# Expert stage of a four-layer network: tiles of 128 tokens, chunks of 256, and weighting dealt between the one-hot instructions

## The chip, the cores and the metric

The kernel runs on one core of one Trainium2 chip. A core has TensorE (PE, matrix products; its weight loads are PEld), VectorE (DVE), ScalarE (ACT), GpSimd (POOL) and SyncE (SP, which issues transfers). Each engine has its own list of instructions, in a written order, and engines wait for each other by semaphores. The metric is the device time of one execution in microseconds (us). The text calls TensorE's two clock levels 1.2 and 2.4 GHz; the profile writes them as a granted clock of 0.50 and 1.00.

## The reference, cut to what matters

The network has 3136 tokens (16 images of 14x14) of 256 channels and four layers. The change lies in the feed-forward part of the third. For each token and each of 8 heads it makes two lists of 64 scores, takes the 16 best of each, forms the sums of the candidates, takes the 16 best of those, and so picks 16 of 4096 experts for each head. Each expert is a row of `expert_down` and a row of `expert_up`.

```python
q = (x_norm @ wq).reshape(B, T, HEADS, 2, DIM_KEY)
sim = jnp.einsum('bthpd,hkpd->pbthk', q, keys)
s1, i1 = jax.lax.top_k(sim[0], K)
s2, i2 = jax.lax.top_k(sim[1], K)
all_idx = (i1[..., :, None] * NUM_KEYS + i2[..., None, :]).reshape(B, T, HEADS, K * K)
all_scores = (s1[..., :, None] + s2[..., None, :]).reshape(B, T, HEADS, K * K)
final_scores, pk = jax.lax.top_k(all_scores, K)
final_idx = jnp.take_along_axis(all_idx, pk, axis=-1)
hidden = jnp.einsum('btd,bthkd->bthk', x_norm, expert_down[final_idx])
hidden = jax.nn.gelu(hidden, approximate=False) * jax.nn.relu(final_scores)
out = jnp.einsum('bthk,bthkd->btd', hidden, expert_up[final_idx])
```

## The kernel before, in words

The whole stage is `peer_ffn` (lines 1353 to 1844). It gathers no rows of experts. It computes the product of every token with all 4096 experts, as 32 blocks (`J`) of 128, applies Gelu, and multiplies the result by a matrix of weights that is zero but for the picked experts. That matrix is built for each token as a product of one-hot matrices: 128 rows from the code `a`, 32 columns from the code `b`, the weight carried as a high and a low bf16 part.

The tokens come in 14 chunks (`CT`) of 224, each of two tiles (`TT`) of 112 tokens and four half tiles (`HT`) of 56 tokens. In a tile, tokens lie on partitions, so that one instruction of the search works on 112 tokens. In what follows chunk n is in work, and the codes of chunk n+1 are searched in the same time. The order on each engine, for chunk n:

- PE (line 1577): `hidden` for 10 of 16 pairs of blocks (L1516, 80 matmuls), then `turn` for both tiles, which transposes the codes (L1525) and waits for `codes_ready`, then `hidden` for the other 6 pairs (48), then `queries` of chunk n+1 (L1494, 16). Then `scatter` for half tiles 0 to 3 (L1540 and L1541, two matmuls for each token, so 112 for each), with `scores` of chunk n+1 (L1503, 8) behind half tile 0 and behind half tile 1. Last comes `experts_out` (L1550, 128).
- DVE (line 1827): `low_weights` (L1791), `one_hots` for half tiles 0 to 3 (four instructions each: L1808, L1809 and twice L1812) and `weigh` for half tiles 0 and 1 (L1820, four each, one for each quarter of a half tile). `weigh` stands behind `one_hots` of the next half tile and multiplies Gelu's result by the scattered weights in PSUM. Then `top_halves` for both tiles, `make_codes` (L1728 to L1786), and last the addition to `x` (L1843).
- ACT: Gelu (L1617), the copies of transposed codes (L1628 to L1630), queries and scores (L1597, L1603), and the copies of the scattered weights of half tiles 2 and 3 (L1639), which POOL multiplies in (L1482).

`one_hots` of half tile hb writes the buffers `oh_a[hb % 2]`, `oh_h[hb % 2]` and `oh_l[hb % 2]`, so it waits until PE has done the scatter of half tile hb-2 (`m_done`). `scatter` of a half tile waits for `oh_ready`, which the last of the four one-hot instructions sets. The function `chunks` (line 1433) writes out the first two and the last two chunks, and puts the others into a loop of two chunks for each turn.

Of the kernel before, what the change touches and what calls it, by code (L numbers as in the profile page):

```python
# [1352 lines left out]
def peer_ffn(nc, x, xn_dram, w, ident):  # L1353
# [10 lines left out]
    TT = 112  # L1364
# [8 lines left out]
    GT = HT // 4  # L1373
    LOWEST = -3.4028235e38
# [4 lines left out]
    with Scope(nc, "peer") as S:  # L1379
# [107 lines left out]
        def _(pe):  # L1487
            def queries(n, p):
# [3 lines left out]
                for m in range(4):  # L1492
                    for k in range(KC):
                        mm = nc.tensor.matmul(sim_ps[m // 2][:, (m % 2) * CT:(m % 2 + 1) * CT], wq[:, k, m * P:(m + 1) * P],  # L1494
                                              xc[p][:, k, :], start=(k == 0), stop=(k == KC - 1))
                mm.then_inc(q_done, 1)

            def scores(n, t):
# [731 lines left out]
```

## Time and profile before

| | |
|---|---|
| median of 3 runs | 2701.39 us (2698.59 to 2703.5) |
| the profiled execution, its own time | 2689.78 us |
| its span, first to last instruction | 2688.1 us |
| mean granted TensorE clock | 0.82 |
| busy: PE, PEld, DVE, ACT, POOL | 2236.6, 1940.0, 1847.0, 663.9, 435.8 us |
| 14 chunks of the expert stage, first transpose of codes to last addition | 676.0 to 2095.7 us |

The busy time of an engine is the union of its instructions. Matmuls are pipelined, so that a stretch in which PE is always busy may still hold more or fewer of them. Start times from instruction to instruction say more than durations. A stretch of the span is named by its start and end in us.

### The profile page before, as it was taken

What the parts mean: (1) busy time and instruction counts of PE and PEld (TensorE: products, weight loads), DVE (VectorE), ACT (ScalarE), POOL (GpSimd) and SP (SyncE); (2) the same over time, 40 slices, a digit from 0 to 9 for tenths busy, and PEclk for the clock granted to TensorE, in tenths of its full rate; (3) what the DMA queues carried; (4) which work ended last, traced back from release to release, by engine and by line L of the source; (5) the groups of instructions that cost most, each with busy time, mean ns of one, the idle gap of its engine ahead of it and who ended that gap; (6) DMA issues with size and microseconds to landing.
All of it is one profiled execution on the core that took longest, in us unless ns stands there. A gap on an engine that the chain in (4) does not pass through costs nothing. (4 is left out here: it accounts for less than half of the span.)

```text
span 2688.1 us, 50156 instructions
## 1 busy us (share of the span) xinstructions
PE 2236.6 (83%) x18017; PEld 1940.0 (72%) x18017; DVE 1847.0 (69%) x7732; ACT 663.9 (25%) x1527; POOL 435.8 (16%) x521
## 2 busy tenths in 40 slices
PE   6585999955989889989989889989888799648994
PEld 3464788734889788888989889889888577326663
DVE  4334666448889889898898898898895577440003
ACT  1432455432211111211211211111111255402220
POOL 2003444310101201102102012012012310030003
PEclk8777999966788697787787887887786799869996
DMA  1104444225000000000000000000000233042323
GB/s 53 34 18 98 106 108 99 47 73 118 5 4 1 5 5 2 5 5 2 5 1 5 5 1 5 5 1 5 1 1 1 65 83 81 7 165 82 104 92 102
DMA packets 87043, 107.85 MB, mean 40 GB/s; under 512 B 26222, under 2 KB 75502, under 8 KB 86062
## 3 DMA queue, kind: packets, MB, share of 16 engines
q1 hardware_dynamic: 81328, 96.62, 13.7%
q0 software_dynamic: 3296, 6.43, 0.9%
q8 instruction: 146, 2.39, 0.4%
q10 hardware_dynamic: 2176, 1.61, 0.2%
q14 instruction: 97, 0.79, 0.1%
HBM read 70.61 MB, written 30.51 MB: 38 GB/s over the span
## 5 line engine op out<-in xcount | busy, mean ns | idle before, releaser
L1540 PE MATMUL peer_x_ps<-peer_oh_h,peer_oh_a 128*128 128x32 bf16 x3136 | 417.2, 249 | 6.1 <-DVE peer_oh_l L1812 4.4
L1540 PEld LDWEIGHTS peer_x_ps<-peer_oh_h,peer_oh_a 128*128 128x128 bf16 x3136 | 414.2, 149 | 8.5 <-DVE peer_oh_l L1812 5.7
L1541 PE MATMUL peer_x_ps<-peer_oh_l,peer_oh_a 128*128 128x32 bf16 x3136 | 417.8, 249 | 0.0
L1541 PEld LDWEIGHTS peer_x_ps<-peer_oh_l,peer_oh_a 128*128 128x128 bf16 x3136 | 412.9, 149 | 3.6 <-issue 1.5
L1516 PE MATMUL peer_x_ps<-peer_xc,peer_dt 128*128 128x224 f32 x1792 | 374.4, 373 | 31.7 <-DMA peer_up<-in_L_ffn_expert_up_dram 19.4
L1482 POOL TENSOR_TENSOR peer_g<-peer_g,peer_qt 128x448 f32<-128x448 f32 x112 | 189.7, 1715 | 1275.0 <-ACT peer_qt L1639 1274.9
L1550 PE MATMUL peer_out_ps<-peer_g,peer_up 128*128 128x224 f32 x1792 | 370.9, 372 | 30.6 <-issue 28.4
L1516 PEld LDWEIGHTS peer_x_ps<-peer_xc,peer_dt 128*128 128x128 f32 x1792 | 362.1, 204 | 40.0 <-issue 34.6
L1550 PEld LDWEIGHTS peer_out_ps<-peer_g,peer_up 128*128 128x128 f32 x1792 | 361.1, 203 | 37.6 <-issue 32.4
L1617 ACT ACTIVATE peer_g<-peer_x_ps 128x448 f32<-128x448 f32 x224 | 121.9, 544 | 652.1 <-PE peer_x_ps L1516 652.1
L1277 DVE TENSOR_REDUCE l_attn_mx<-l_attn_s_ps 98x4 f32<-98x392 f32 (+1 forms) x320 | 175.0, 560 | 140.4 <-PE l_attn_s_ps L1047 100.6
L1808 DVE TENSOR_TENSOR peer_oh_a<-peer_a_t,peer_iota_f 128x7168 bf16<-128x7168 bf16 x56 | 217.6, 3886 | 1.4
L1662 DVE FIND_INDEX8 peer_i<-peer_v,peer_sc 112x8 uint32<-112x64 f32 x896 | 186.4, 220 | 0.0
L1198 ACT ACTIVATE l_attn_pt<-l_attn_st_ps 98x392 f32<-98x392 f32 x320 | 148.2, 492 | 151.2 <-PE l_attn_st_ps L1060 150.4
L2165 DVE TENSOR_TENSOR moe_y<-moe_y_ps,moe_b 98x256 f32<-98x256 f32 x32 | 13.6, 425 | 222.8 <-PE moe_y_ps L2039 222.8
L1043 PE MATMUL l_attn_s_ps<-l_attn_stk,l_attn_stq 96*98 96x196 bf16 (+1 forms) x768 | 112.8, 244 | 27.5 <-DMA l_attn_stk<-l_attn_pieces_k_dram 15.6
L1820 DVE TENSOR_TENSOR peer_g<-peer_g,peer_x_ps 128x448 f32<-128x448 f32 x112 | 67.6, 620 | 94.6 <-PE peer_x_ps L1541 94.5
L1657 DVE MAX8 peer_v<-peer_sc 112x8 f32<-112x64 f32 x896 | 118.7, 209 | 11.3 <-issue 10.1
L972 POOL TENSOR_SCALAR_AFFINE_SELECT l_attn_pt<-l_attn_pt 98x196 f32<-98x196 f32 (+1 forms) x192 | 98.5, 518 | 140.9 <-ACT l_attn_pt L1198 139.5
L1060 PE MATMUL l_attn_st_ps<-l_attn_stq,l_attn_stk 98*98 98x196 bf16 (+1 forms) x768 | 112.7, 245 | 10.2 <-ACT l_attn_pt L1198 4.4
L2039 PE MATMUL moe_y_ps<-moe_w,moe_h 128*98 128x256 f32 x512 | 111.8, 379 | 0.0
L2039 PEld LDWEIGHTS moe_y_ps<-moe_w,moe_h 128*98 128x98 f32 x512 | 84.5, 165 | 27.6 <-issue 1.3
(308 smaller groups left out, 3633.5 us busy)
## 6 DMA issues: line engine op xcount, KB each, us to landing
moe_w<-in_L_ffn_w_dram SPq DMA_DIRECT2D x16, 1024.0 KB, 9.1
l_attn_pieces_q_dram<-l_attn_pieces_q SPq DMA_DIRECT2D x16, 294.0 KB, 3.9
l_attn_pieces_k_dram<-l_attn_pieces_k SPq DMA_DIRECT2D x16, 294.0 KB, 3.1
l_attn_stq<-l_attn_pieces_q_dram SPq DMA_DIRECT2D x16, 294.0 KB
l_attn_stk<-l_attn_pieces_k_dram SPq DMA_DIRECT2D x16, 294.0 KB
peer_g<-n_L_ffn_expert_down_dram SPq DMA_DIRECT2D x8, 512.0 KB, 6.7
peer_up<-in_L_ffn_expert_up_dram SPq DMA_DIRECT2D x2, 2048.0 KB
l_xi<-net_x SPq DMA_DIRECT2D x16, 196.0 KB, 2.3
```

The lines of the kernel that those rows point to most:

```text
L1198: nc.scalar.activation(pt[g % NPT][:, f * FW:(f + 1) * FW], st_ps[i % 2][0:TH, 0:FW], ACT.Exp).then_inc(exp_done, 1)
L1277: nc.vector.tensor_reduce(mx[n % 2][:, hs[0]:hs[0] + len(hs), t], s_ps[i % 2][0:TH, 0:FW].rearrange("p (h j) -> p h j", j=nb * TH), AX_X, ...
L1482: nc.gpsimd.tensor_tensor(g[:, :, ts], g[:, :, ts], m_copy[q % 2].rearrange("p (t j) -> p j t", j=J), ALU.mult).then_inc(g_done_late, 1)
L1516: mm = nc.tensor.matmul(x_ps[b][:, jj * CT:(jj + 1) * CT], dt[:, k, 2 * jp + jj, :], xc[p][:, k, :], start=(k == 0), stop=(k == KC - 1))
L1540: nc.tensor.matmul(x_ps[q][:, i * J:(i + 1) * J], oh_a[hb % 2][:, :, t], oh_h[hb % 2][:, :, t], start=True, stop=False)
L1541: mm = nc.tensor.matmul(x_ps[q][:, i * J:(i + 1) * J], oh_a[hb % 2][:, :, t], oh_l[hb % 2][:, :, t], start=False, stop=True)
L1550: mm = nc.tensor.matmul(out_ps[:, m * CT:(m + 1) * CT], up[:, j, m * P:(m + 1) * P], g[:, j, :], start=(j == 0), stop=(j == J - 1))
L1617: nc.scalar.activation(g[:, 2 * jp:2 * jp + 2, :], x_ps[jp % 4][:, 0:2 * CT].rearrange("p (j t) -> p j t", j=2), ACT.Gelu).then_inc(gelu_d ...
L1657: ins = nc.vector.max(values[:, q, r], source)
L1662: last = nc.vector.max_index(indices[:, q, r], values[:, q, r], source)
L1808: nc.vector.tensor_tensor(view(oh_a[q]), spread(a_t, P), number(P), ALU.is_equal)
L2039: mm = nc.tensor.matmul(y_ps[s % 2][0:ST, 0:C], h[p][:, f, s * ST:(s + 1) * ST], w2[p][:, f, :], start=(f == 0), stop=(f == KF - 1))
```

## The change

Tiles have 128 tokens, half tiles 64, chunks 256. 3136 tokens are 12 such chunks and a rest of 64, which is a 13th chunk of one half tile: all functions are given the number of tokens of the chunk in work (`now`) and of the one that is searched (`then`). The loop holds chunks 2 to 9 (four turns; before, chunks 2 to 11 in five).

For room, the small buffers of `make_codes` (`t1`, `f16`, `step16` and others) now lie behind the selection matrices in `oh_a`. The wait for all scatters of the chunk in work (`m_done`) therefore stands at the head of `make_codes`, where it stood behind its search before.

The four `weigh` instructions of half tile hb-1 no longer follow `one_hots` of half tile hb. They stand between and behind its four instructions. The core of the diff:

```diff
-    TT = 112
+    TT = 128
...
+    REST = NT - NCHUNK * CT
...
-        f16, p16 = S.sb("f16", [TT, HH, TOP]), S.sb("p16", [TT, HH, TOP], U32)
-        t1, t2, t3 = S.sb("t1", [TT, PP]), S.sb("t2", [TT, PP]), S.sb("t3", [TT, PP])
+        def behind(p, word, words, dt):
+
+            o = TOP * PP + 2 * word
+            return flat[p][:, o:o + 2 * words].bitcast(dt)
+
+        t1, t2, t3 = (behind(0, i * PP, PP, F32) for i in range(3))
...
             for p in range(2):
-                chunk(NCHUNK - 2 + p, p, p == 1)
+                chunk(NCHUNK - 2 + p, p, CT, CT if p == 0 else REST)
+            chunk(NCHUNK, 0, REST, 0)
+
+        def tile_rows(tokens):
+
+            return [min(TT, tokens - t0) for t0 in range(0, tokens, TT)]
...
-            def chunk(n, p, last):
-                hidden(n, p, range(EARLY))
-                for t in range(NTILE):
-                    turn(n, t)
-                hidden(n, p, range(EARLY, NPAIR))
-                if not last:
-                    queries(n + 1, 1 - p)
-                for hb in range(NHB):
+            def chunk(n, p, now, then):
+                hidden(n, p, range(EARLY), now)
+                for t, rows in enumerate(tile_rows(now)):
+                    turn(n, t, rows)
+                hidden(n, p, range(EARLY, NPAIR), now)
+                if then > 0:
+                    queries(n + 1, 1 - p, then)
+                next_rows = tile_rows(then)
+                for hb in range(now // HT):
                     scatter(n, hb)
-                    if hb < NTILE and not last:
-                        scores(n + 1, hb)
-                experts_out(n)
+                    if hb < len(next_rows):
+                        scores(n + 1, hb, next_rows[hb])
+                experts_out(n, now)
...
-            def make_codes(n):
-
+            def make_codes(n, tiles):
+
+                heads, rows = len(tiles) * NH, tiles[0]
                 v = v16[:, :, :].rearrange("t (h w) a -> t w h a", w=2)
                 o = 0
                 chain.wait()
+                wait(dve, m_done, 4 * NHB * n)
...
-                wait(dve, m_done, 4 * NHB * n)
...
             def one_hots(n, hb):
+
+                def weigh_last(quarter):
+                    if 0 < hb <= LATE:
+                        weigh(n, hb - 1, quarter)
...
                 nc.vector.tensor_tensor(view(oh_a[q]), spread(a_t, P), number(P), ALU.is_equal)
+                weigh_last(0)
                 chain.step(nc.vector.tensor_tensor(view(oh_l[q]), spread(b_t, J), number(J), ALU.is_equal))
+                weigh_last(1)
                 chain.wait()
-                for dst, wt in ((oh_h, wh_t), (oh_l, wl_t)):
-                    ins = nc.vector.tensor_tensor(dst[q][:, :, :], oh_l[q][:, :, :], wt[:, ts].unsqueeze(1).broadcast_to([P, J, HT]), ALU.mult)
-                ins.then_inc(oh_ready, 1)
-
-            def weigh(n, hb):
-
-                for q in range(4):
-                    dve.wait_ge(m_done, 4 * NHB * n + 4 * hb + q + 1)
...
+                nc.vector.tensor_tensor(oh_h[q][:, :, :], oh_l[q][:, :, :], wh_t[:, ts].unsqueeze(1).broadcast_to([P, J, HT]), ALU.mult)
+                weigh_last(2)
+                nc.vector.tensor_tensor(oh_l[q][:, :, :], oh_l[q][:, :, :], wl_t[:, ts].unsqueeze(1).broadcast_to([P, J, HT]),
+                                        ALU.mult).then_inc(oh_ready, 1)
+                weigh_last(3)
+
+            def weigh(n, hb, q):
+
+                dve.wait_ge(m_done, 4 * NHB * n + 4 * hb + q + 1)
...
-                for hb in range(NHB - 1):
-                    one_hots(n, hb + 1)
-                    if hb < LATE:
-                        weigh(n, hb)
...
+                for hb in range(n_hb):
+                    if hb + 1 < n_hb:
+                        one_hots(n, hb + 1)
```

DVE, the first chunk before, from the one-hot instructions of half tile 1 to those of half tile 2 (the last numbers are partitions and elements; `x4` are four in a row):

```order
L1808 TENSOR_TENSOR peer_oh_a<-peer_a_t,peer_iota_f 128x7168
L1809 TENSOR_TENSOR peer_oh_l<-peer_b_t,peer_iota_f 128x1792
L1812 TENSOR_TENSOR peer_oh_h<-peer_oh_l,peer_wh_t 128x1792
L1812 TENSOR_TENSOR peer_oh_l<-peer_oh_l,peer_wl_t 128x1792
L1820 TENSOR_TENSOR peer_g<-peer_g,peer_x_ps 128x32x14 x4
L1808 TENSOR_TENSOR peer_oh_a<-peer_a_t,peer_iota_f 128x7168
L1809 TENSOR_TENSOR peer_oh_l<-peer_b_t,peer_iota_f 128x1792
```

The same place on DVE in the changed kernel, where L1833 to L1840 are the one-hot instructions and L1848 is `weigh`:

```order
L1833 TENSOR_TENSOR peer_oh_a<-peer_a_t,peer_iota_f 128x8192
L1848 TENSOR_TENSOR peer_g<-peer_g,peer_x_ps 128x32x16
L1835 TENSOR_TENSOR peer_oh_l<-peer_b_t,peer_iota_f 128x2048
L1848 TENSOR_TENSOR peer_g<-peer_g,peer_x_ps 128x32x16
L1838 TENSOR_TENSOR peer_oh_h<-peer_oh_l,peer_wh_t 128x2048
L1848 TENSOR_TENSOR peer_g<-peer_g,peer_x_ps 128x32x16
L1840 TENSOR_TENSOR peer_oh_l<-peer_oh_l,peer_wl_t 128x2048
L1848 TENSOR_TENSOR peer_g<-peer_g,peer_x_ps 128x32x16
L1833 TENSOR_TENSOR peer_oh_a<-peer_a_t,peer_iota_f 128x8192
L1848 TENSOR_TENSOR peer_g<-peer_g,peer_x_ps 128x32x16
```

The four multiplications of half tile 0 have moved up between the one-hot instructions of half tile 1, and those of half tile 1 up into half tile 2. The instruction that sets `oh_ready` (L1840) now stands behind three of them.

DVE, the end of the stage in the changed kernel, which is all of its work for the 13th chunk from the one-hot instructions on:

```order
L1833 TENSOR_TENSOR peer_oh_a<-peer_a_t,peer_iota_f 128x8192
L1835 TENSOR_TENSOR peer_oh_l<-peer_b_t,peer_iota_f 128x2048
L1838 TENSOR_TENSOR peer_oh_h<-peer_oh_l,peer_wh_t 128x2048
L1840 TENSOR_TENSOR peer_oh_l<-peer_oh_l,peer_wl_t 128x2048
L1848 TENSOR_TENSOR peer_g<-peer_g,peer_x_ps 128x32x16 x4
L1875 TENSOR_TENSOR net_x<-net_x,peer_out_ps 128x2x64
```

Here the four multiplications stand together, and the addition covers 64 tokens.

## Rows read from the trace of the kernel before

**Rows 1.** Waits of the expert stage, 680 to 2030: us in total, times, longest.

```profile
DVE peer_g L1820 <- PE peer_x_ps L1541: 89.8, 71, 3.3
PE peer_tr_ps L1525 <- DVE peer_codes L1786: 73.2, 12, 8.1
```

**Rows 2.** DVE's stages: us, busy PE, PEld, DVE, ACT, POOL (instructions), clock, DMA, GB/s.

```profile
1192.89:1227.49 34.60, 33.45 (x304) 31.98 (x305) 26.27 (x23) 6.50 (x16) 0.00 (x0) 0.75 0.03 8
1227.49:1235.75 8.26, 8.26 (x101) 7.64 (x101) 8.22 (x5) 2.48 (x5) 3.34 (x2) 0.71 0.00 0
1235.75:1263.42 27.67, 25.46 (x206) 24.76 (x205) 27.41 (x265) 3.00 (x6) 10.21 (x7) 0.69 0.01 2
1263.42:1266.48 3.06, 3.06 (x18) 3.06 (x17) 2.99 (x10) 0.00 (x0) 0.00 (x0) 1.00 0.00 0
1266.48:1280.39 13.91, 11.09 (x51) 10.22 (x50) 13.75 (x133) 0.00 (x0) 0.00 (x0) 0.87 0.02 4
1280.39:1295.76 15.37, 15.36 (x73) 14.68 (x71) 15.04 (x29) 4.90 (x9) 0.00 (x0) 0.89 0.00 1
```

**Rows 3.** The same chunk by PE's stages: us, PE busy (instructions), clock, DMA, GB/s.

```profile
1192.89:1195.45 2.56, 1.41 (x7) 0.50 0.00 0
1195.45:1205.96 10.51, 10.51 (x50) 0.86 0.01 2
1205.96:1208.99 3.03, 3.03 (x17) 1.00 0.31 76
1208.99:1216.36 7.37, 7.37 (x113) 0.70 0.01 2
1216.36:1219.35 2.99, 2.99 (x12) 0.59 0.00 0
...
1229.66:1244.57 14.91, 14.91 (x225) 0.59 0.01 2
1244.57:1246.78 2.21, 0.00 (x1) 0.50 0.00 0
1246.78:1274.26 27.48, 27.48 (x128) 0.89 0.01 2
1274.26:1295.75 21.49, 18.67 (x81) 0.84 0.01 2
...
1298.69:1307.78 9.09, 9.09 (x50) 1.00 0.01 2
```

**Rows 4.** PE over 13 chunks and over the last one.

```profile
676.00:2016.67 1340.67, 1209.14 (x9646) 0.80 0.01 3
2016.67:2095.70 79.03, 69.05 (x630) 0.71 0.00 1
```

**Rows 5.** DVE timeline, one-hot instructions of half tile 3: start, us.

```profile
1227.49 3.88 DVE L1808 TENSOR_TENSOR peer_oh_a<-peer_a_t,peer_iota_f 128x7168 bf16<-128x7168 bf16 x1
1231.29 1.08 DVE L1809 TENSOR_TENSOR peer_oh_l<-peer_b_t,peer_iota_f 128x1792 bf16<-128x1792 bf16 x1
1232.41 1.09 DVE L1812 TENSOR_TENSOR peer_oh_h<-peer_oh_l,peer_wh_t 128x1792 bf16<-128x1792 bf16 x1
1233.42 2.40 DVE L1812 TENSOR_TENSOR peer_oh_l<-peer_oh_l,peer_wl_t 128x1792 bf16<-128x1792 bf16 x1
```

**Rows 6.** POOL timeline in the same stretch: start, us, how many, idle before.

```profile
1232.41 10.71 POOL L1482 TENSOR_TENSOR peer_g<-peer_g,peer_qt 128x448 f32<-128x448 f32 x6 [88.37 <-ACT peer_qt L1639]
```

**Rows 7.** DVE by form, two stretches: the same shape on 112 and on 98 partitions.

```profile
L1757 DVE TENSOR_TENSOR peer_t<-peer_t 112x256 f32<-112x256 f32 x11 | 4.6, 419 | 0.0
L2165 DVE TENSOR_TENSOR moe_y<-moe_y_ps,moe_b 98x256 f32<-98x256 f32 x10 | 4.2, 425 | 93.6 <-PE moe_y_ps L2039 93.6
```

**Rows 8.** PE timeline: 80 matmuls of `hidden` where no loop turns.

```profile
1374.74 15.30 PE L1516 MATMUL peer_x_ps<-peer_xc,peer_dt 128*128 128x224 f32 x80
```

**Rows 9.** PE, L1571 alone (16 matmuls, 128 weights, 128 columns, f32): us, busy, clock last.

```profile
618.01:619.65 1.64, 1.64 (x16) 1.64 (x15) 1.00 0.00 0
```

**Rows 10.** PE, L1043 alone (98 weights side by side, 98 columns, bf16).

```profile
249.00:249.19 0.19, 0.18 (x4) 0.18 (x3) 1.00 0.61 186
```

More of the change, by code:

```diff
@@ L1618, in hidden_out, with chunk @@
                                          ACT.Gelu).then_inc(gelu_done, 1)
-            def chunk(n, p, last):
+            def chunk(n, p, now, then):
                 wait(act, out_done, n)
-                hidden_out(n, range(EARLY))
-                for t in range(NTILE):
+                hidden_out(n, range(EARLY), now)
+                for t, rows in enumerate(tile_rows(now)):
                     act.wait_ge(tr_done, NTILE * n + t + 1)
-                    ts = slice(t * TT, (t + 1) * TT)
+                    ts = slice(t * TT, t * TT + rows)
@@ L1636, in chunk @@
-                for k in range(4 * (NHB - LATE)):
+                    nc.scalar.activation(wh_t[:, ts], tr_ps[:, 2 * TT:2 * TT + rows], ACT.Copy)
+                    nc.scalar.activation(a_t[:, ts], tr_ps[:, 0:rows], ACT.Copy)
+                    nc.scalar.activation(b_t[:, ts], tr_ps[:, TT:TT + rows], ACT.Copy).then_inc(tr_ready, 1)
+                hidden_out(n, range(EARLY, NPAIR), now)
+                if then > 0:
+                    query_out(n + 1, then)
+                    for t, rows in enumerate(tile_rows(then)):
+                        score_out(n + 1, t, rows)
@@ L1637, in chunk @@
+                for k in range(4 * max(0, now // HT - LATE)):
                     act.wait_ge(m_done, 4 * NHB * n + 4 * LATE + k + 1)
@@ L1702, in fold, with top_halves @@
                 else:
[L1703 to L1705 removed]
+                    chain.step(nc.vector.tensor_tensor(out, m[:, 0, :], m[:, 1, :], ALU.add))
+            def top_halves(n, t, rows):
                 dve.wait_ge(sim_ready, NTILE * n + t + 1)
@@ L1823, in _, with chunk @@
             for t in range(NTILE):
[L1824 to L1828 removed]
+                top_halves(0, t, TT)
+            make_codes(0, tile_rows(CT))
+            def chunk(n, p, now, then):
+                if p == 0 and now == CT:
                     chain.turn(n, 2)
[L1830 removed]
+                tiles, n_hb = tile_rows(now), now // HT
+                low_weights(n, 0, tiles[0])
                 one_hots(n, 0)
[L1832 to L1840 removed]
+                if len(tiles) > 1:
+                    low_weights(n, 1, tiles[1])
+                for hb in range(n_hb):
+                    if hb + 1 < n_hb:
+                        one_hots(n, hb + 1)
+                if n_hb == 1:
+                    for q in range(4):
+                        weigh(n, 0, q)
+                if then > 0:
+                    for t, rows in enumerate(tile_rows(then)):
+                        top_halves(n + 1, t, rows)
+                    make_codes(n + 1, tile_rows(then))
```

143 lines of the change are left out of this document (66 added, 77 removed).

## The prediction

> **What bounds the kernel now.** I read the waits of the expert stage first, then one chunk cut into DVE's stages, then the same chunk cut into PE's. The waits point both ways [rows 1]: PE waits for DVE's codes, 73.2 us in 12 waits, and DVE's `weigh` waits for PE's scatter, 89.8 us in 71. So neither engine is the bound by itself. The stages show a circle through both [rows 2, 3]. From the first transpose of the codes (1192.89) PE sets the pace: transposes 2.56, the rest of `hidden` 10.51, queries 3.03, scatter of half tile 0 7.37, scores 2.99, scatter of half tile 1 7.4. DVE has its one-hot matrices ready beside it, and ends the last `weigh` at 1227.49, about 0.8 behind the scatter. From there DVE sets the pace alone: one-hots of half tile 3 (8.26, they wait for the buffer that scatter 1 frees), the search in the halves (27.67), candidates (3.06), their search (13.91), codes (15.37). The circle is 34.60 + 68.27 = 102.87 us. All 13 intervals take 1340.67 us, 103.1 each, and what follows the last transposes 79.03 [rows 4]: 1419.7 us in all. PE's own work ends earlier than the codes, which is why it waits.
>
> **The change, part by part.**
>
> *Search on 128 partitions.* The instructions, their count and their elements per partition are the same; only partitions go from 112 to 128. The same shape takes 419 ns on 112 and 425 ns on 98 partitions [rows 7], so partitions cost nothing, and the 27.67 + 3.06 + 13.91 + 15.37 = 60.0 us stay 60.0 us for a chunk that is 8/7 as large. This is the gain. The buffers that now lie in `oh_a` are read and written at the same sizes; I charge nothing.
>
> *One-hot matrices of 64 tokens.* Everything on DVE that grows with tokens: 7168 elements start 3.80 us before the next instruction (1231.29 less 1227.49) and 1792 elements about 1.1 [rows 5]. One seventh more of both, fixed part left out, is 0.53 + 3 x 0.13 = 0.93 us a half tile. The last instruction took 2.40 instead of 1.09, 1.31 more, while POOL worked [rows 5, 6]. POOL now has its first work about 5.2 us after that half tile begins (4.92 before, plus a longer quarter of scatter and copy), and the two multiplications start at 5.6 and later, so that either one or both meet it. A meeting costs 1.31 to 1.5. Bounds 9.2 (no longer meeting than now) and 10.9 (two); I take 10.2.
>
> In rows 5 and 6 POOL's first instruction starts with one DVE multiplication and the next one is the long one. The Trainium skill ("SBUF — State Buffer", section "SBUF: two separate sides") says that a DVE instruction with two SBUF inputs and a GpSimd instruction reading SBUF lock each other out for the whole instruction. By that rule both multiplications would be held, 10.9 instead of 10.2, or 8 us more over the stage; the row shows one held of two in the old spacing, so the midpoint stands.
>
> *PE's part of the circle.* Matmuls of 256 columns instead of 224 and 128 instead of 112 for each half tile: hidden, queries and two scatters grow by 1/7. In rows 3, 9.09 us (clock 1.00) against 10.51 (0.86) is `hidden` without and with the clock lost in the wait for codes. With the level kept: transposes 2.7, hidden 10.4, queries 3.46, scatter 2 x 8.42, scores 3.1 (256 columns before and after), tail 0.85: 37.4. With it lost, 38.8. PE will idle about 3 us instead of 9 there, so I take 37.9. The circle is 37.9 + 10.2 + 60.0 + 0.2 = 108.3 us for 256 tokens, where 103.1 x 8/7 would be 117.8.
>
> *Weighing dealt between the one-hots.* I cost it at nothing. `weigh` of quarter q cannot start before that quarter is scattered, and `one_hots` of half tile 2 cannot start before scatter 0 has ended, since it reuses its buffer. Both ends are PE's. Let scatter 0 start at S. The dealt `weigh` instructions run at about S+2.3, 4.4, 6.5 and 8.6 with one-hot work between them, and DVE is free for half tile 2 at S+9.3, dealt or not. The waits of rows 1 stay, they only stand between other instructions. The price is in `oh_ready`: half tile 1 was ready before the scatter began, and now at S+8.4, behind three waits. Queued behind it is the scatter of half tile 1, which PE reaches after scores at S+11.5: 3.1 us of cover, without which each us late costs 12 us in all. Half tile 2 is ready 3.1 us ahead likewise; half tile 3 (10.2 after scatter 1 and its tail 0.85) is due 11.5 after it, margin 0.5, and is not on DVE's chain. Bounds: 0 and 1 us a chunk.
>
> *The wait for `m_done` moved to the head of `make_codes`.* PE ends scatter 3 at 1244.57, DVE begins there at 1263.42 [rows 2, 3]; afterwards the ends are some 20 us and 38 us behind scatter 1. 18 us of cover: nothing. The wait for `tr_done` stays.
>
> *PE becomes nearly as long as DVE.* From scatter 1's end: 37.1 + scores 3.1 + scatters 17.0 + POOL's last product 2.4 + experts_out 30 (27.48 less the 3.3 it loses at half clock, by 8/7, plus 3.3, and a us less in most chunks) + 80 hidden 17.3 = 106.9, against 108.3. The wait for codes shrinks to some 1.4 us. At a loop's turn PE loses more: `hidden` took 21.49 us from 1274.26 to 1295.75 instead of 15.30 [rows 3, 8], 6.2 more, 2.8 of it idle (21.49 less 18.67) and the rest clock (0.84). I take 5.3, since a shorter idle costs less clock. That was hidden by the wait for codes. Now 106.9 + 5.3 = 112.2 exceeds 108.3 by 3.9. There are three such turns (four before), 12 us. Bounds: 2.2 and 5 each.
>
> *The last, small chunk.* Chunk 11 searches only 64 tokens (half the instructions), so PE bounds it: 37.1 less 1.7 for short queries, no second scores, 17.0 + 2.4 + 30, then 80 matmuls with 64 columns. The trace has none; 128 columns with 128 weights take 1.64/16 = 0.10 us [rows 9], and 98 weights with 98 columns in bf16 0.047 [rows 10]. I take 0.109 (0.05 to 0.21, the half clock): 8.7. Sum 93.5. Then transposes and copies 1.6, one-hots 8.0, one scatter 8.4, `weigh` 0.9, 128 such matmuls 14 and a start at half clock 2.4, addition 0.3: 35.5 after 79.03.
>
> *Sum.* 11 x 108.3 + 12 + 93.5 + 35.5 = 1332.3 us against 1419.7: 87.4 less. The profiled execution of 2689.78 would become 2602.4. It lies 11.6 under the median of the runs shown, so for the median 2701.4 - 87.4 = 2614 us.
>
> **The rivals.**
>
> *A faster circle.* The clock stays up, POOL meets one instruction, turns cost 2.2: 11 x 107.0 + 6.6 + 91 + 33 = 1307.6, 112 less, 2589. If, beyond that, dealing took DVE's waits out, 89.8 us less, 2500; what speaks against it is that PE's scatter ends them. Two in a hundred for the latter.
>
> *PE's turn in the circle.* PE idles less, but if it loses clock at more places or POOL ends late, it is at 112 in every chunk: 11 x 112 + 93.5 + 35.5 = 1361, 59 less, 2643. For it: only 1.4 us separates the engines. Against: a busier PE held 1.00 in `hidden` when it had not waited [rows 3].
>
> *The search pays for partitions.* Then the 60.0 us become 68.6, the circle 116.9, and the stage 1332 + 95 = 1427: nothing gained, 2709. Rows 7 speak against it; 3 in 100.
>
> *Slower: the scatter's weights.* L1540 loads 128 weights of `oh_a` whose step goes from 56 to 64 elements, 112 to 128 bytes. It takes 7.37/112 = 66 ns at a granted clock of 0.70 and 14.91/224 = 67 ns at 0.59 [rows 3], so array clock does not set its pace, and weights side by side take 0.19/4 = 47 ns [rows 10]. Something in fetching or issuing them does, and it might dislike the round step. From both sides: 47 ns, and 103 to 109 ns (rows 9) as the slow end. At 109 PE has 512 x 0.043 = 22 us more: 129 a chunk, 11 x 129 + 12 + 115 + 41 = 1587, 167 more, 2869. It decides from a chunk of about 116.2 us, that is from 66 + 18 = 84 ns. At 47 ns the circle would shorten by 256 x 0.019 = 5. For it: the unexplained 66 ns. Against: 112 bytes are already a jump at every element. I take 66, the row of the same instruction.
>
> Beside this: the Trainium skill ("SBUF — State Buffer", section "Door 1: The DMA port swizzle") states 16-byte lines and a penalty for each access that leaves one. By it both steps pay the same and this rival is void; no run so far shows a step of 128 bytes.
>
> **How the numbers follow.** My forecast with its own range (2590 to 2635) 0.68; faster circle below that 0.06; PE at 112 or thereabouts 0.16; search pays for partitions 0.03 (half of it within 0.2%, half slower); slower scatter 0.05; other things 0.02. The time is 2614, the range 2588 to 2646: it takes in the third case and leaves out the last three. A measurement of this kernel cannot tell less than about 0.2%, 5 us, from nothing. Faster 0.91, the same 0.03, slower 0.06.
>
> **What would show it.** In the changed kernel's profile: first transposes of codes every 108 us or so, 112 at a loop's turn; L1678, L1683 and L1685 at 209 to 220 ns on 128 partitions; 128 scatter matmuls in 8.4 us; DVE's waits in `weigh` about as long a chunk as before (7 us); PE's wait for codes down from 6.1 us each to under 2. Wrong would be: the scatter over 8.8 us, scatter 1 or 2 waiting for L1840, `hidden` at a clock under 0.9 everywhere, or DVE waiting less for PE with an earlier end of scatter 1.

## The result, and the profile after

| | before | changed |
|---|---|---|
| median of the runs (lowest to highest), us | 2699.99 (2695.79 to 2703.5), 4 runs | 2795.77 (2790.82 to 2804.15), 4 runs |
| profiled execution / its span, us | 2689.78 / 2688.1 | 2790.82 / 2789.1 |
| expert stage, first transpose of codes to last addition, us | 1419.7 | 1523.0 |
| mean start to start of a scatter matmul, ns | 65.7 | 98.6 |

The ratio is 1.0368, with a 95% interval of 1.0344 to 1.0392: 3.7% slower, where 3.2% faster was forecast. In the profiled executions the stage is 103.3 us longer and the spans differ by 101.0, so the loss lies in the expert stage.

The waits tell it first. These are those of the changed kernel, 660 to 2130 (engine, what, line, released by what: us in total, times, longest), beside [rows 1]:

```profile
DVE peer_g L1848 <- PE peer_x_ps L1559: 174.2, 96, 5.2
PE peer_tr_ps L1543 <- DVE peer_wl_t L1812: 15.4, 12, 1.3
```

PE waits no longer for the search: of the 73.2 us behind `codes` nothing is left, only 1.3 us a chunk behind `low_weights`, between two transposes. DVE waits twice as long for PE. The bound has gone over to PE altogether. What PE does with the time stands in one chunk cut into PE's stages (us, PE busy and instructions, clock, DMA, GB/s), beside [rows 3]:

```profile
1275.98:1278.27 2.29, 1.00 (x8) 1.00 0.00 0
1278.27:1288.47 10.20, 10.20 (x49) 1.00 0.01 2
1288.47:1291.92 3.45, 3.45 (x17) 1.00 0.29 76
1291.92:1304.48 12.56, 12.56 (x130) 0.61 0.01 1
1304.48:1308.03 3.55, 3.55 (x10) 0.50 0.00 0
1308.03:1320.65 12.62, 12.62 (x129) 0.64 0.01 1
1324.20:1349.60 25.40, 25.40 (x257) 0.57 0.01 1
1349.68:1352.07 2.39, 0.01 (x2) 0.50 0.00 0
1352.07:1381.75 29.68, 29.68 (x128) 0.93 0.01 1
1381.95:1401.98 20.03, 17.61 (x81) 1.00 0.01 3
```

In order: transposes, the rest of `hidden`, queries, scatter of half tile 0, scores, scatter 1, then scatters 2 and 3, the wait for POOL's last product, experts_out, and `hidden` of the next chunk with a loop's turn in it. Everything but the scatter and the loop's turn lies within half a us of the forecast (2.7, 10.4, 3.46, 3.1 for scores, 2.4, 30); the turn's `hidden` was forecast at 17.3 + 5.3 = 22.6 and took 20.03. A scatter of 128 pairs takes 12.6 us, not 8.42: 98 ns for a pair of a weight load and a matmul. The profile's page has them in groups, one for each of the two matmuls of a token, of which the first is shown, and DVE's large one-hot instruction (busy us, mean ns of one, idle before):

```profile
L1558 PEld LDWEIGHTS peer_x_ps<-peer_oh_h,peer_oh_a 128*128 128x128 bf16 x3136 | 619.9, 235 | 6.5 <-DVE peer_oh_l L1840 3.5
L1558 PE MATMUL peer_x_ps<-peer_oh_h,peer_oh_a 128*128 128x32 bf16 x3136 | 621.6, 291 | 3.4 <-DVE peer_oh_l L1840 3.4
L1833 DVE TENSOR_TENSOR peer_oh_a<-peer_a_t,peer_iota_f 128x8192 bf16<-128x8192 bf16 x49 | 216.6, 4420 | 1.3
```

The matmul has 32 columns and 128 weights, as before; what is new in it is the step at which the weights are read, 128 bytes instead of 112, and with it the step of the 32 moving columns. (LDWEIGHTS overlap each other and the matmuls, so I go by the start-to-start time of the pairs.) The sum follows: a chunk's PE work was forecast at 106.9 us, and 512 pairs at 98.6 - 66 = 32.6 ns more make 123.6; the intervals between the first transposes of two chunks measure 122.7 to 123.2, and 125.8 to 126.1 at the three loop turns.

Two other causes can be looked at in the same trace, the clock and DVE's writes. The first 2 us of scatter 0 lie wholly at one clock level and its second half and more at the other (us, PE busy and instructions, clock, DMA, GB/s):

```profile
1291.92:1293.92 2.00, 2.00 (x23) 1.00 0.00 0
1295.92:1304.00 8.08, 8.08 (x86) 0.50 0.00 0
```

From start to start the matmuls take 95 ns in the first and 98 in the second. The last chunk has one scatter with DVE nearly idle (us; busy PE, PEld, DVE, ACT, POOL; clock, DMA, GB/s):

```profile
2140.00:2152.96 12.96, 12.96 (x128) 12.84 (x128) 2.08 (x3) 0.00 (x0) 0.00 (x0) 0.50 0.00 1
```

That is 101 ns a pair (12.96/128) at half clock with DVE busy 2.08 of 12.96 us, and 98 at a clock of 0.61 to 0.64 with DVE at work. Neither the clock nor DVE's writes can be much of it.

The dealing, on DVE's timeline from the scatter of half tile 0 (start, us, instruction, idle before and its releaser):

```profile
1295.24 0.69 DVE L1848 TENSOR_TENSOR peer_g<-peer_g,peer_x_ps 128x512 f32<-128x512 f32 x1 [5.05 <-PE peer_x_ps L1559]
1295.85 1.22 DVE L1835 TENSOR_TENSOR peer_oh_l<-peer_b_t,peer_iota_f 128x2048 bf16<-128x2048 bf16 x1
1298.39 0.70 DVE L1848 TENSOR_TENSOR peer_g<-peer_g,peer_x_ps 128x512 f32<-128x512 f32 x1 [1.33 <-PE peer_x_ps L1559]
1299.01 1.22 DVE L1838 TENSOR_TENSOR peer_oh_h<-peer_oh_l,peer_wh_t 128x2048 bf16<-128x2048 bf16 x1
1301.49 0.69 DVE L1848 TENSOR_TENSOR peer_g<-peer_g,peer_x_ps 128x512 f32<-128x512 f32 x1 [1.27 <-PE peer_x_ps L1559]
1302.10 1.22 DVE L1840 TENSOR_TENSOR peer_oh_l<-peer_oh_l,peer_wl_t 128x2048 bf16<-128x2048 bf16 x1
1304.69 0.69 DVE L1848 TENSOR_TENSOR peer_g<-peer_g,peer_x_ps 128x512 f32<-128x512 f32 x1 [1.37 <-PE peer_x_ps L1559]
```

All four `weigh` end a wait for PE, with one-hot work between them, as forecast; `oh_l` of half tile 1 is ready at 1303.3, and its scatter begins at 1308.03.

### The profile page after: what moved, and what is told of

Read it like the earlier page. It is cut to its first block and busy times, and to the rows that moved or that the text cites. A ratio compares the mean times of both kernels' runs of the same rounds, so it can differ in the third digit from the quotient of the medians.

```text
span 2789.1 us, 48544 instructions
## 1 busy us (share of the span) xinstructions
PE 2410.7 (86%) x17712; PEld 2047.9 (73%) x17712; DVE 1750.2 (63%) x7060; ACT 658.0 (24%) x1478; POOL 413.2 (15%) x505
## 5 line engine op out<-in xcount | busy, mean ns | idle before, releaser
L1558 PEld LDWEIGHTS peer_x_ps<-peer_oh_h,peer_oh_a 128*128 128x128 bf16 x3136 | 619.9, 235 | 6.5 <-DVE peer_oh_l L1840 3.5
L1558 PE MATMUL peer_x_ps<-peer_oh_h,peer_oh_a 128*128 128x32 bf16 x3136 | 621.6, 291 | 3.4 <-DVE peer_oh_l L1840 3.4
L1559 PEld LDWEIGHTS peer_x_ps<-peer_oh_l,peer_oh_a 128*128 128x128 bf16 x3136 | 619.4, 236 | 5.9 <-issue 5.3
L1559 PE MATMUL peer_x_ps<-peer_oh_l,peer_oh_a 128*128 128x32 bf16 x3136 | 621.6, 289 | 0.0
L1569 PE MATMUL peer_out_ps<-peer_g,peer_up 128*128 128x256 f32 (+1 forms) x1664 | 386.8, 401 | 29.3 <-issue 26.2
L1534 PE MATMUL peer_x_ps<-peer_xc,peer_dt 128*128 128x256 f32 (+1 forms) x1664 | 352.5, 372 | 27.5 <-DMA peer_up<-in_L_ffn_expert_up_dram 19.7
L1500 POOL TENSOR_TENSOR peer_g<-peer_g,peer_qt 128x512 f32<-128x512 f32 x96 | 170.4, 1775 | 1335.7 <-ACT peer_qt L1660 1335.7
L1638 ACT ACTIVATE peer_g<-peer_x_ps 128x512 f32<-128x512 f32 (+1 forms) x208 | 119.1, 572 | 643.6 <-PE peer_x_ps L1534 643.6
L1833 DVE TENSOR_TENSOR peer_oh_a<-peer_a_t,peer_iota_f 128x8192 bf16<-128x8192 bf16 x49 | 216.6, 4420 | 1.3
L1848 DVE TENSOR_TENSOR peer_g<-peer_g,peer_x_ps 128x512 f32<-128x512 f32 x100 | 69.3, 693 | 185.2 <-PE peer_x_ps L1559 185.2
L1683 DVE FIND_INDEX8 peer_i<-peer_v,peer_sc 128x8 uint32<-128x64 f32 (+1 forms) x800 | 167.2, 221 | 0.0
L1043 PE MATMUL l_attn_s_ps<-l_attn_stk,l_attn_stq 96*98 96x196 bf16 (+1 forms) x768 | 113.1, 244 | 28.4 <-DMA l_attn_stk<-l_attn_pieces_k_dram 17.3
L1678 DVE MAX8 peer_v<-peer_sc 128x8 f32<-128x64 f32 (+1 forms) x800 | 106.9, 213 | 10.9 <-issue 9.8
```

Source lines behind the costliest of these rows:

```text
L1043: mm = nc.tensor.matmul(out[:, j, :], stq[n % NB][0:KS, spot(h), t * TH:(t + 1) * TH], stk[n % NB][0:KS, spot(h), 0:nb * TH], start=(j == ...
L1500: nc.gpsimd.tensor_tensor(g[:, :, ts], g[:, :, ts], m_copy[q % 2].rearrange("p (t j) -> p j t", j=J), ALU.mult).then_inc(g_done_late, 1)
L1534: mm = nc.tensor.matmul(x_ps[b][:, jj * CT:jj * CT + cols], dt[:, k, 2 * jp + jj, :], xc[p][:, k, 0:cols], start=(k == 0), stop=(k == KC - 1))
L1558: nc.tensor.matmul(x_ps[q][:, i * J:(i + 1) * J], oh_a[hb % 2][:, :, t], oh_h[hb % 2][:, :, t], start=True, stop=False)
L1559: mm = nc.tensor.matmul(x_ps[q][:, i * J:(i + 1) * J], oh_a[hb % 2][:, :, t], oh_l[hb % 2][:, :, t], start=False, stop=True)
L1569: mm = nc.tensor.matmul(out_ps[:, m * CT:m * CT + cols], up[:, j, m * P:(m + 1) * P], g[:, j, 0:cols], start=(j == 0), stop=(j == J - 1))
```

## The experiments

**The theory**: the step of the scatter's weights, 128 bytes, is what costs 33 ns a pair, and the rest of the change gains what was forecast. **The rivals**: the moving operand (`oh_h`, `oh_l`), whose step also became 128 bytes; the dealing; the larger tile or the moved buffers as such. The pads below widen a row's step in memory and move the buffers behind it; the same elements are written and read.

| run | tokens a tile | step of weights, of moving, bytes | `weigh` | ns a pair | stage, us | time against before [95%] |
|---|---|---|---|---|---|---|
| before | 112 | 112, 112 | behind | 65.7 | 1419.7 | 1 |
| changed | 128 | 128, 128 | dealt | 98.6 | 1523.0 | 1.0368 [1.0344, 1.0392] |
| e1 | 112 | 128, 112 | dealt | 90.9 | 1476.9 | 1.0199 [1.0164, 1.0234] |
| e2 | 128 | 132, 128 | dealt | 62.5 | 1310.7 | 0.9593 [0.9558, 0.9627] |
| e3 | 128 | 128, 132 | dealt | 90.4 | 1477.5 | 1.0210 [1.0176, 1.0245] |
| e4 | 128 | 128, 128 | behind | 98.6 | 1523.4 | 1.0361 [1.0333, 1.0390] |
| e5 | 128 | 132, 132 | dealt | 63.5 | 1313.7 | 0.9582 [0.9549, 0.9615] |
| e6 | 128 | 132, 128 | behind | 62.4 | 1314.8 | 0.9590 [0.9543, 0.9638] |
| e7 | 112 | 132, 112 | dealt | 65.2 | 1423.3 | 1.0002 [0.9985, 1.0020] |
| e8 | 112 | 144, 112 | dealt | 60.4 | 1405.8 | one run: 2683.72 us, before 2698.97 |
| e9 | 128 | 136, 128 | dealt | 63.6 | 1314.2 | 0.9606 [0.9561, 0.9652] |
| e10 | 112 | 160, 112 | dealt | 79.8 | 1462.7 | one run: 2719.66 us, before 2685.17 |
| e11 | 112 | 136, 112 | dealt | 65.1 | 1425.5 | one run: 2696.61 us, before 2685.17 |
| e12 | 128 | 144, 128 | dealt | 63.5 | 1313.6 | 0.9592 [0.9567, 0.9618] |

"ns a pair" is the mean start-to-start time of the scatter's matmuls in the profiled execution. A single run may lie half a per cent off (the runs of before beside e10 and e11 span 2670.75 to 2693.76 us), so for e8, e10 and e11 the pace and the stage are what is read.

**e1_step64_tiles112**: the changed kernel taken back to tiles of 112, with the step alone put to 128 bytes.

```diff
-    TT = 128
+    TT = 112
...
-        oh_a = [S.sb(f"oh_a{p}", [P, P, HT], BF16) for p in range(2)]
+        STEP_A = 64
+        oh_w = [S.sb(f"oh_a{p}", [P, P, STEP_A], BF16) for p in range(2)]
+        oh_a = [m[:, :, 0:HT] for m in oh_w]
...
-            chunk(NCHUNK, 0, REST, 0)
```

> Edit: the changed kernel put back to tiles of 112 and chunks of 224 (14 chunks, no rest), with the rows of oh_a kept 64 elements (128 bytes) apart, of which 56 are used. Theory 1 (the step of the scatter's weights): a scatter matmul starts every 99 ns instead of 66, a half tile takes 11.0 us instead of 7.4, a chunk 103.1 + 7.4 = 110.5 us or a little more, the time is 2700 + 14 x 7.4 = about 2805 us. Theory 2 (something about half tiles of 64 tokens: full PSUM banks, 128 partitions, the small 13th chunk): 66 ns and 2700 us. Theory 3 (the step of the moving operands oh_h and oh_l, which stays at 112 bytes here): 66 ns and 2700 us.

Measured: 90.9 ns, 1.0199. One scatter of 112 pairs, where before took 7.37 [rows 3]:

```profile
1211.18:1221.34 10.16, 10.16 (x114) 0.67 0.01 2
```

The step alone slows the scatter, at the old tile size. The time came out at 2734.83 us, where the expectation had 99 ns and 2805. The stage loses 57 us and not the whole 112 x 4 x 25 ns = 11.3 us a chunk, because before PE still had about 6 us a chunk of waiting for codes to give. But 90.9 is not 98.6: a part is missing.

**e2_weights_step66**: the changed kernel, weights off the step.

```diff
-        oh_a = [S.sb(f"oh_a{p}", [P, P, HT], BF16) for p in range(2)]
+        STEP_A = 66
+        oh_w = [S.sb(f"oh_a{p}", [P, P, STEP_A], BF16) for p in range(2)]
+        oh_a = [m[:, :, 0:HT] for m in oh_w]
...
-        flat = [oh_a[p][0:TT, :, :].rearrange("t r k -> t (r k)") for p in range(2)]
+        flat = [oh_w[p][0:TT, :, :].rearrange("t r k -> t (r k)") for p in range(2)]
```

(`GI = 8` columns of `iota_f` instead of 16, or 14 at tiles of 112, make room for the pad, here and in e3, e5, e6, e9, e10 and e12. DVE's one-hot instruction takes 4420 ns with either, and e3, which has the same 8 columns, stays slow.)

> Edit: the changed kernel with the rows of oh_a 66 elements (132 bytes) apart, 64 used; to make room iota_f holds 8 columns instead of 16 and is read twice as often by the one-hot comparison. Theory 1: the scatter is back at about 66 ns a matmul (8.4 us a half tile) and the time near my forecast, 2614 us, in any case 2590 to 2646. Theory 2: 99 ns, 12.7 us a half tile, 2796 us. Theory 3: the same as theory 2.

Measured: 62.5 ns, 0.9593, 4.1% faster than before. Four bytes more between two weights turn the change from a loss into a gain. The expectation had 66 ns and 2590 to 2646 us. The pace is a little better than that, and 2572.14 us lies below the range; before took 2685.21 us beside it, and 0.9593 of the 2699.99 us above is 2590. The same stages of one chunk of e2 as were shown of the changed kernel:

```profile
1192.06:1194.17 2.11, 0.91 (x7) 1.00 0.00 0
1194.17:1204.55 10.38, 10.38 (x51) 1.00 0.01 2
1204.55:1208.00 3.45, 3.45 (x17) 1.00 0.28 76
1208.00:1215.95 7.95, 7.95 (x129) 0.78 0.01 2
1215.95:1219.37 3.42, 3.42 (x11) 0.52 0.00 0
1219.37:1227.37 8.00, 8.00 (x130) 0.70 0.01 2
1230.92:1247.14 16.22, 16.22 (x257) 0.50 0.00 2
1249.52:1279.12 29.60, 29.60 (x129) 0.94 0.01 2
1279.12:1298.86 19.74, 17.54 (x82) 1.00 0.01 2
```

Only the scatter differs: 7.95 and 8.00 for 12.56 and 12.62, 16.22 for 25.40. It does so at clocks of 0.78, 0.70 and 0.50, at the same 62 to 63 ns a pair.

**e3_moving_step66**: weights at 128 bytes, the moving operand off the step.

```diff
-        oh_h = [S.sb(f"oh_h{p}", [P, J, HT], BF16) for p in range(2)]
+        oh_h = [S.sb(f"oh_h{p}", [P, J, 66], BF16)[:, :, 0:HT] for p in range(2)]
```

(and `oh_l` alike)

> Edit: the changed kernel with the rows of oh_h and oh_l (the scatter's moving operands, 32 columns) 66 elements apart and oh_a left at 64; iota_f of 8 columns as in the kernel with weights at 66. Theory 1: no change against the changed kernel, 99 ns and 2796 us, since weights are 128 of the 160 elements that a matmul fetches. Theory 3: 66 ns and about 2614 us. If both operands matter in proportion, some 93 ns and 2775 us.

Measured: 90.4 ns, 1.0210, which is e1's pace. One scatter of 128 pairs:

```profile
1169.75:1181.32 11.57, 11.57 (x129) 0.65 0.01 1
```

The expectation of the first theory, no change, failed: the moving operand's step costs 8 ns a pair too, and this is the part missing in e1, whose moving operand stayed at 112 bytes. So of the 33 ns, 25 come with the step of the weights alone (e1) and 8 with both steps at 128 bytes.

**e4_no_deal**: the changed kernel with `weigh` of half tiles 0 and 1 put back behind the next one-hots.

```diff
-                    if 0 < hb <= LATE:
-                        weigh(n, hb - 1, quarter)
+                    pass
...
+                        if hb < LATE:
+                            for q in range(4):
+                                weigh(n, hb, q)
```

> Edit: the changed kernel with the four weighing multiplications back behind the one-hot instructions of the next half tile, everything else as changed. Theory 1 and my account of the dealing (PE's scatter ends both orders): no change, 2796 us within 5. Rival, dealing costs time because oh_ready comes late and PE waits for it: 5 to 20 us less than the changed kernel. Rival, dealing saves time: more than 2800.

Measured: 1.0361 [1.0333, 1.0390] beside 1.0368 [1.0344, 1.0392] of the changed kernel; DVE waits 183.5 us in `weigh` over the span instead of 185.2. The dealing does nothing while PE is the bound.

**e5_both_step66** (the diffs of e2 and e3 together) and **e6_step66_no_deal** (those of e2 and e4).

> Edit: as the kernel with weights at 66 elements, and the rows of oh_h and oh_l 66 apart as well. So far: weights and moving operand both at 128 bytes 99 ns, moving operand alone moved off 91, weights alone moved off 62.5. If the two costs add up: 62.5 less 8 = about 54 ns a scatter matmul, and some 512 x 0.008 = 4 us less a chunk for PE. If the scatter is limited by something else once the weights are off 128 bytes: 62 ns and the time of the kernel with weights alone at 66, within 5 us.

> Edit: weights at 66 elements, and the weighing multiplications back behind the one-hot instructions. Here DVE and PE are within 1 to 2 us of each other in a chunk, so the dealing can show. My account (scatter ends both orders): the same time as with dealing, within 4 us, and the same wait of DVE for PE in a chunk. Rival, dealing pays because DVE's waits go: 10 us or more slower without it. Rival, dealing costs through the late oh_ready: 5 us or more faster without it.

Measured: 63.5 ns, 0.9582, and 62.4 ns, 0.9590; both intervals hold e2's 0.9593. So the moving operand's step costs something only when the weights' step is 128 bytes as well; an effect that adds up would have given 54 ns. And the dealing is worth nothing at the better step either: DVE idles 70.6 us before `weigh` without it and 70.4 with it.

**e7_tiles112_step66** (e1 with `STEP_A = 66`) and **e8_tiles112_step72** (`STEP_A = 72`).

> Edit: tiles of 112 and chunks of 224 as before, weights at 66 elements (132 bytes) instead of 56 (112 bytes), buffers and dealing as changed. If 132 bytes give 62.5 ns here as well, two scatters in the circle are 0.8 us shorter, the stage some 11 us, and the kernel is 0.4% faster than before. Then the tiles of 128 are worth some 97 us by themselves. If the pace of 62.5 came from the larger tiles: 66 ns and the time of before.

> Edit: as the kernel with tiles of 112 and step 66, but 72 elements (144 bytes). If only a step of a whole 128 bytes is slow: 62 to 66 ns. If the pace gets worse with the power of two in the step (112 and 144 bytes are odd multiples of 16, 132 of 4): 66 ns as at 112 bytes, not 62.5.

Measured: 65.2 ns and exactly the time of before, 1.0002 [0.9985, 1.0020]; and 60.4 ns. e7 has the moved buffers, the moved `m_done` wait and the dealing, and differs from e2 in the tile size and what hangs on it: these other edits together are worth 0, and the tile size, with the small gain in pace that came with it, is worth 1423.3 - 1310.7 = 112.6 us of the stage. That e7 would reach e2's 62.5 ns failed: it keeps the 65 ns of 112-byte steps. e8's scatter, in a row:

```profile
1195.17:1201.93 6.76, 6.76 (x114) 0.74 0.01 2
```

6.76 us for 112 pairs, the fastest of all, and faster than either branch of its expectation (62 to 66 ns, or 66).

**e9_tiles128_step68**, **e10_tiles112_step80**, **e11_tiles112_step68**, **e12_tiles128_step72**: the curve of pace against the step. e12 had to find 2 x 2 KB more in each partition, and put `codes` into the second matrix's tail:

```diff
-        codes = S.sb("codes", [TT, 3, PP])
+        codes = behind(1, 3 * PP, 3 * PP, F32).rearrange("t (s k) -> t s k", s=3)
```

> Edit: the changed kernel with the weights' rows 68 elements (136 bytes) apart, iota_f of 8 columns, dealt order. So far at tiles of 128: 128 bytes 98.6 ns, 132 bytes 62.5. At tiles of 112: 112 bytes 65.7, 128 bytes 90.9, 132 bytes 65.2, 144 bytes 60.4. If only whole multiples of 128 bytes are slow: 60 to 66 ns, and a stage of 1300 to 1315 us, 0.96 of the time before. If a step shared with 8 bytes already costs: over 70 ns.

> Edit: as the kernel with tiles of 112 and step 72, but 80 elements (160 bytes, 5 x 32), and iota_f of 8 columns. If only a whole 128 bytes is slow: 60 to 66 ns. If the cost grows with the power of two in the step (144 is an odd multiple of 16, 160 of 32, 128 of itself): between 60 and 91, some 70 ns.

> Edit: as the kernel with tiles of 112 and step 72, but 68 elements (136 bytes). If odd multiples of 16 bytes are the best steps and 4 bytes is not (132 gave 65.2, 144 gave 60.4): 62 to 64 ns. If the step does not matter away from 128 and the 60.4 was the run: 65 ns.

> Edit: the changed kernel with the weights' rows 72 elements (144 bytes) apart; the codes buffer moved behind the selection matrix in the second oh_a and iota_f of 8 columns, to make room. 144 bytes gave 60.4 ns at tiles of 112. If that holds with half tiles of 64: 7.7 us a half tile, two of them in the circle 0.5 us shorter than with 132 bytes, a stage of 1300 to 1306 us and 0.955 to 0.958 of the time before. If 60.4 was particular to the other size: 62 to 64 ns and 0.959 to 0.961.

Measured: 63.6, 79.8, 65.1 and 63.5 ns. e10's and e12's scatters:

```profile
1208.47:1217.38 8.91, 8.91 (x113) 0.67 0.01 2
```

```profile
1210.53:1218.71 8.18, 8.18 (x130) 0.67 0.01 2
```

e9 and e11 fell in a branch of their expectations each; e10's 80 ns are above the 70 that were expected, inside the 60 to 91 given with them. 160 bytes are slow too, so it is no penalty of 128 alone, and not of the step's length, as 144 is no slower than 112. By the power of two in the step the runs line up, which is an order among six steps and not a cause that was tested: 128 (128 x 1) takes 90 to 99, 160 (32 x 5) 80, and 144 and 112 (16 x 9, 16 x 7), 136 (8 x 17) and 132 (4 x 33) 60 to 66. e12 did not carry e8's 60.4 over to tiles of 128: it took 63.5 ns, and 0.9592, the branch of its expectation without that gain.

The versions that beat both kernels are e2, e5, e6, e9 and e12, at 0.958 to 0.961 of before, with intervals that overlap: each of the steps 132, 136 and 144 does. The simplest is e2, 2572.14 us where before took 2685.21 beside it.

## Why the prediction was wrong

**The step that failed** is the price of the scatter: "At 47 ns the circle would shorten by 256 x 0.019 = 5. ... I take 66, the row of the same instruction." The row was of the same instruction at another step, and the step is what the change altered. The prediction had named the mechanism as its slower rival, drew the point from which it decides (84 ns) and gave it 5 in 100. What came was 98.6 ns, within its 47 to 109. Its reason against it, that "112 bytes are already a jump at every element", is refuted by e1 and e7: at 112 tokens a tile, a jump of 132 bytes costs the 65 ns of one of 112, and one of 128 costs 91. What counts is which jump. The Trainium skill ("SBUF — State Buffer", section "Door 1: The DMA port swizzle") has a penalty for each access that crosses to a new 16-byte line, and no further one for a particular larger step. Taken as the full account, by which 112 and 128 bytes pay alike, it does not hold for these weight loads: every step here leaves the line at every element, and they run from 60 to 99 ns.

What the runs showed in its place: 25 ns more a pair from the weights' step alone (e1 at 90.9 beside 65.7), 8 more with the moving operand's step, and with both a PE cycle of 123 us that nothing covers, where 106.9 was forecast under a circle of 108.3. The prediction's own sign of being wrong, a scatter over 8.8 us, came at 12.56. The row that should have given it more weight was in hand: 66 ns at two clock levels, above the 47 of another matmul with weights side by side, said that something other than the array's clock set the pace, and nothing in the trace bounded it at a new step.

The other terms, read from e2, which differs from the changed kernel in that step:

- *Circle, 108.3 us a chunk and 12 us for turns*: e2's first eleven intervals take 1168.7 us (658.19 to 1826.91), where 11 x 108.3 + 12 = 1203.3 were forecast, 34.6 too many. PE's part of the circle, first transposes to the one-hots of half tile 3, is 36.1 for 37.9 (1192.06 to 1228.18), and 18.5 less over the eleven. The scatter at 62.5 and transposes of 2.11 for 2.7 are in it, and a clock that holds 1.00 in `hidden`. One-hots of half tile 3 take 9.28 (1228.18 to 1237.46) for 10.2, and 6.1 less over the eleven. The other 10.0 are the turns, forecast at 12, with what else varies.
- *POOL's meeting*: a mixture. In eight of the eleven chunks of e2 one instruction is held, as before, and the one-hots take 9.27 to 9.29 us, the forecast's lower bound; in three both are held, and they take 10.58 to 10.68. The mean is 9.65, where 10.2 was taken. (The upper bound of 10.9 was itself mis-added: 9.2 and one more meeting of 1.31 to 1.5 is at most 10.7.) The usual case in e2:

```profile
1233.77 1.23 DVE L1841 TENSOR_TENSOR peer_oh_h<-peer_oh_l,peer_wh_t 128x2048 bf16<-128x2048 bf16 x1
1234.91 2.62 DVE L1843 TENSOR_TENSOR peer_oh_l<-peer_oh_l,peer_wl_t 128x2048 bf16<-128x2048 bf16 x1
```

```profile
1233.91 9.82 POOL L1503 TENSOR_TENSOR peer_g<-peer_g,peer_qt 128x512 f32<-128x512 f32 x5 [89.92 <-ACT peer_qt L1663]
```

  The first multiplication starts 0.14 us before POOL and takes 1.23; the second starts beside POOL's work and takes 2.62. It is the picture of [rows 5, 6]. Three chunks of e2 have POOL first, here by 0.12 us, and then both are held:

```profile
1021.16 2.56 DVE L1841 TENSOR_TENSOR peer_oh_h<-peer_oh_l,peer_wh_t 128x2048 bf16<-128x2048 bf16 x1
1023.65 2.63 DVE L1843 TENSOR_TENSOR peer_oh_l<-peer_oh_l,peer_wl_t 128x2048 bf16<-128x2048 bf16 x1
```

```profile
1021.04 1.60 POOL L1503 TENSOR_TENSOR peer_g<-peer_g,peer_qt 128x512 f32<-128x512 f32 x1 [92.79 <-ACT peer_qt L1663]
```

  In the changed kernel the slower scatter brings POOL one instruction later, and there POOL pays:

```profile
1328.21 1.22 DVE L1840 TENSOR_TENSOR peer_oh_l<-peer_oh_l,peer_wl_t 128x2048 bf16<-128x2048 bf16 x1
```

```profile
1328.35 2.65 POOL L1500 TENSOR_TENSOR peer_g<-peer_g,peer_qt 128x512 f32<-128x512 f32 x1 [99.57 <-ACT peer_qt L1660]
1331.42 1.69 POOL L1500 TENSOR_TENSOR peer_g<-peer_g,peer_qt 128x512 f32<-128x512 f32 x1 [0.42 <-ACT peer_qt L1660]
```

  DVE, first by 0.14 us, keeps its 1.22; POOL's product takes 2.65 where its next takes 1.69. The one that comes second is held. The rule of the Trainium skill ("SBUF — State Buffer", section "SBUF: two separate sides") is that whichever of the two starts first has the shared port pair for its whole instruction. I had read it as holding both multiplications always; by its wording the first is held only where POOL has started before it, and all these rows agree.
- *Search on 128 partitions costs nothing*: right. From the first `MAX8` of the search to the next chunk's first transpose takes 59.9 to 60.1 us in e2 where no loop turns, and 60.0 to 60.3 in before. The two search instructions that weigh most, in before on 112 partitions (680 to 2030):

```profile
L1662 DVE FIND_INDEX8 peer_i<-peer_v,peer_sc 112x8 uint32<-112x64 f32 x832 | 173.1, 220 | 0.0
L1657 DVE MAX8 peer_v<-peer_sc 112x8 f32<-112x64 f32 x832 | 110.2, 209 | 1.1
```

  and in e2 on 128 partitions and, for the small chunk, on 64 (680 to 1900):

```profile
L1686 DVE FIND_INDEX8 peer_i<-peer_v,peer_sc 128x8 uint32<-128x64 f32 x704 | 145.7, 218 | 0.0
L1681 DVE MAX8 peer_v<-peer_sc 128x8 f32<-128x64 f32 x704 | 93.2, 208 | 0.9
...
L1686 DVE FIND_INDEX8 peer_i<-peer_v,peer_sc 64x8 uint32<-64x64 f32 x32 | 6.4, 209 | 0.0
L1681 DVE MAX8 peer_v<-peer_sc 64x8 f32<-64x64 f32 x32 | 4.2, 200 | 0.0
```

  The same on 112 and 128, and on half of 128 only 4% less. This is where most of the 112.6 us between e7 and e2 come from; the 2.7 ns a pair between the two runs are in them as well.
- *PE nearly as long as DVE*: right. The forecast's PE cycle of 106.9 stands beside e2's intervals of 104.7 to 109.3, and the wait for `codes` [rows 1] fell from 73.2 us to 8.3, less than the 1.4 a chunk of the forecast. In e2's waits (us, times, longest):

```profile
PE peer_tr_ps L1546 <- DVE peer_codes L1810: 8.3, 6, 2.1
```

- *A loop's turn, 5.3*: `hidden` takes 19.74 in e2 and 20.03 in the changed kernel with the turn, 17.43 without, so 2.3 to 2.6 and up to 3.1 in other chunks. It kept its clock of 1.00 in both, so the half that I put on the clock was not there. PE no longer waits for codes next to it, but no run shows that this is why.
- *Dealing and moved wait, nothing*: right (e4, e6, e7).
- *The small chunk and the end, 93.5 + 35.5*: e2 took 95.8 + 46.2. The matmuls of 64 columns were nearly right in `hidden` and wrong in experts_out:

```profile
1913.78:1922.75 8.97, 8.97 (x81) 8.90 (x79) 0.69 (x1) 2.49 (x9) 0.00 (x0) 1.00 0.01 2
1941.04:1968.61 27.57, 27.57 (x128) 27.38 (x128) 0.00 (x0) 0.00 (x0) 0.00 (x0) 0.50 0.00 1
```

  80 in 8.97 us at a clock of 1.00, 0.112 each (0.109 forecast); 128 in 27.57 at 0.50, 0.215 each, as the upper bound had it. I had charged 14 us at full clock and 2.4 for a start at half clock, a figure that stands in no row; here the clock did not come back in 27.57 us: 11.2 too few.

Together -34.6 + 2.3 + 10.7 = -21.6 us, and 1332.3 - 21.6 = 1310.7 is e2's stage. So the forecast's sum was too high by 22 us for e2, and by 17 to 19 for e5, e6, e9 and e12, whose weights are off 128 bytes too, and 190.7 us too low for the kernel as it was changed. The case of "PE's turn in the circle" at 112 did not come in e2: a busier PE kept its clock of 1.00 in `hidden`. Its picture, PE as the bound in every chunk, is what the changed kernel shows, at 123 and by way of the scatter.

**What stays open.** Why the step matters is not shown: the runs show an order by the power of two in the step, which would fit a memory that is divided in some way, but no run looks into it. The pads also move the buffers behind them, and no run moves a buffer at an unchanged step; the pace went with the step in every placement that was run, at 128 bytes in the changed kernel, e1 and e3. Open too is why a moving operand at 128 bytes adds 8 ns only beside weights at 128. The Trainium skill ("TensorE: Matmul & The Clock Gate", section "Step-by-step: what each phase is for") says that the loading of the next weights takes no read bandwidth from the running matmul; e3 against the changed kernel (90.4, 98.6) shows the two operands' steps acting together, so something joins them in this case, and no run shows what. It is also open why 144 bytes gave 60.4 ns at 112 tokens and 63.5 at 128, and what makes the spread of 62 to 66 among the others. The start of the stage lies between 658 and 678 us in different executions; its cause was not looked for, and stages of two runs are therefore compared rather than their spans.

## What to carry to other kernels

A tile size that is also the inner dimension of a buffer sets the step at which another engine reads it. Before such a change, list every read that jumps by that dimension, and treat its duration as unknown at the new step: a row at the old step is no bound. Where it is a round number (here 128 bytes, and less so 160), try a pad of a few bytes; here 4 bytes behind each 128 turned 3.7% slower into 4.1% faster.

A matmul pace that stays the same at either clock level is a sign in a profile that something other than the array's clock sets it. Here it changed with the step of the operands in memory.

## What the runs showed of the hardware

- Weights in bf16, 128 of them at a fixed step in each partition, each load followed by a matmul of 32 columns: 60 to 66 ns a pair at steps of 112, 132, 136 and 144 bytes, 80 at 160, 90 to 91 at 128, and 98.6 at 128 where the moving operand's step is 128 too. At 132 bytes the pace is the same at granted clocks of 0.50 and 0.78, and at 128 it is 95 ns at 1.00 and 98 at 0.50.
- A DVE multiplication of two SBUF operands and a POOL multiplication in SBUF hold each other up, the later one waiting: DVE 2.56 to 2.63 us for 1.23, POOL 2.65 for 1.69.
- DVE writes into the padded matrices at the same speed: 4420 ns for 8192 elements at steps of 128 and 132 bytes.
- 128 matmuls of 128 weights and 64 columns in f32 took 27.57 us at a clock of 0.50, with PE busy throughout and the clock at its lower level to the end.
